# First attention: the keys' exponentials straight from PSUM, head by head, with the bound as bias

## What is computed

```python
def _feature_map(t, K):
    f = jnp.einsum('hdf,bhld->bhlf', K, t)
    feats = jnp.concatenate([jax.nn.softmax(f, axis=-1), jax.nn.softmax(-f, axis=-1)], axis=-1)
    return jnp.maximum(feats, EPS)          # EPS = 1e-12
q, k, v = _heads(x @ Wq), _heads(x @ Wk), _heads(x @ Wv)   # 16 heads of 64
qf, kf = _feature_map(q, Kq), _feature_map(k, Kk)
kv = jnp.cumsum(kf[:, :, :, None, :] * v[..., None], axis=2)
o = jnp.einsum('bhlf,bhldf->bhld', qf, kv)
z = jnp.einsum('bhlf,bhlf->bhl', qf, jnp.cumsum(kf, axis=2)) + EPS
y = (o / z[..., None]) ... @ Wo
```

## Time and profile before

| | |
|---|---|
| median of 3 runs | 1234.21 us (1233.17 to 1234.81) |
| the profiled execution | 1229.25 us, its span 1227.0 us |
| busy over the span | PE 1117.3 (91%), DVE 962.1 (78%), ACT 611.1 (50%), GpSimd 377.3 (31%) |
| granted TensorE clock, mean | 0.982 |
| first attention, tiles 0 to 15 | about 53 to 540 us |

### The profile page before, as it was taken

The page is one execution under the profiler, slowest core; times in us unless marked ns, Lnnn a source line. Parts: engine busy times, 40 slices in busy tenths (PEclk is TensorE's granted clock), DMA queues, the critical chain, the costliest instruction groups (busy, mean ns, idle before and its releaser), DMA issues. The chain is left out here.

```text
span 1227.0 us, 30062 instructions
## 1 busy us (share of the span) xinstructions
PE 1117.3 (91%) x11860; PEld 719.6 (59%) x11861; DVE 962.1 (78%) x1769; ACT 611.1 (50%) x1166; POOL 377.3 (31%) x355
## 2 busy tenths in 40 slices
PE   6698898899899999879999999999999957999996
PEld 5577777777788878643443344334444334666765
DVE  6889978987888788888788677877889556777757
ACT  4233343334333433227777677776788822444443
POOL 4432245222522222113201320222110414656651
PEclk9899999999999999999999999999999988999998
DMA  7100001000400000524720570065050144221225
GB/s 240 41 8 1 2 28 53 2 1 1 80 2 2 1 1 2 81 59 81 152 34 8 114 146 2 9 127 108 2 211 3 53 80 145 65 64 60 63 62 205
DMA packets 60045, 73.65 MB, mean 60 GB/s; under 512 B 14404, under 2 KB 51140, under 8 KB 59188
## 3 DMA queue, kind: packets, MB, share of 16 engines
q1 hardware_dynamic: 56132, 61.56, 21.0%
q0 software_dynamic: 3792, 10.36, 2.7%
HBM read 52.86 MB, written 18.78 MB: 58 GB/s over the span
## 5 line engine op out<-in xcount | busy, mean ns | idle before, releaser
L1791 DVE TENSOR_REDUCE neg_max<-pS 128x1 f32<-128x1024 f32 x238 | 284.9, 1220 | 56.2 <-PE pS L1574 56.0
L1706 ACT ACTIVATE pt<-pR 128x512 f32<-128x512 f32 x512 | 286.5, 600 | 80.1 <-PE pR L1597 75.3
L1597 PE MATMUL pR<-qs,ks 100*32 100x512 bf16 x2048 | 191.2, 383 | 3.1 <-ACT pt L1706 1.6
L1574 PE MATMUL pS<-ks,qs 100*32 100x512 bf16 x1904 | 145.9, 381 | 5.1 <-issue 1.9
L1611 PE MATMUL b_pO<-pt,b_v 128*32 128x512 f32 x1024 | 135.9, 605 | 2.9 <-ACT pt L1706 2.3
L1597 PEld LDWEIGHTS pR<-qs,ks 100*32 100x32 bf16 x2048 | 56.2, 96 | 95.3 <-issue 25.6
L324 POOL TENSOR_TENSOR kf<-kf,fsum 128x2048 f32<-128x2048 f32 (+1 forms) x17 | 58.2, 3422 | 163.8 <-DVE fsum L933 163.8
L324 POOL TENSOR_TENSOR qs<-qs,fsum 128x2048 f32<-128x2048 f32 (+1 forms) x17 | 58.5, 3446 | 142.7 <-DVE fsum L933 142.7
L1453 POOL COPY qs<-max_rows 3x512 bf16<-3x512 bf16 x60 | 36.6, 610 | 209.3 <-ACT max_rows L1699 206.3
L745 ACT COPY qfT<-pT 128x512 f32<-128x512 f32 x64 | 37.3, 582 | 122.7 <-PE pT L466 122.7
L1574 PEld LDWEIGHTS pS<-ks,qs 100*32 100x32 bf16 x1904 | 51.4, 97 | 74.3 <-issue 35.7
(11 more groups left out here) (376 smaller groups left out, 2270.8 us busy)
## 6 DMA issues: line engine op xcount, KB each, us to landing
qs<-q_scr SPq DMA_DIRECT2D x24, 256.0 KB
ks<-k_scr SPq DMA_DIRECT2D x7, 768.0 KB
k_scr<-f SPq DMA_DIRECT2D x18, 256.0 KB, 2.8
ks<-in_L_ffn_w_dram SPq DMA_DIRECT2D x2, 2048.0 KB, 11.1
ks<-in_L_ffn_w_dram SPq DMA_DIRECT2D x4, 1024.0 KB, 8.5
ks<-y_rows SPq DMA_DIRECT2D x16, 256.0 KB, 5.1
ks<-k_scr SPq DMA_DIRECT2D x6, 512.0 KB
cx<-in_ctx_dram SPq DMA_DIRECT2D x3, 768.0 KB, 12.3
```

The costliest lines, as they stand in the source:

```text
L1574: ins = pe.matmul(pS1[q:q + XV, slot, 512 * half:512 * half + 512], qs[0:KR, bass.ds(par, 1), h, P * t + q:P * t + q + XV].rearrange("r a ...
L1597: ins = pe.matmul(ring[bank][q:q + XV, :], ks[0:KR, bass.ds(par, 1), h, P * j + q:P * j + q + XV].rearrange("r a n -> r (a n)"), qs[0:KR, ...
L1706: nc.scalar.activation(pt[:, j % 2, i, :], ring[bank], ACT.Exp).then_inc(exp_done, 1)
L1791: nc.vector.tensor_reduce(neg_max[:, hg % 2, u // G, u % G:u % G + 1], pS1[:, u % 2, :], AX_X, ALU.max, negate=True).then_inc(max_done, 1)
```

## The change

ACT reads the keys' projections from PSUM and takes exp(f - max) and exp(min - f) itself: one instruction for each head and sign, on 128x64, with the negated maximum or the minimum of the head as the bias of each row. That is 32 instructions for a tile in place of two, in four parts of eight. DVE only takes the bounds (`key_bounds`) and shifts no keys. `project_q` waits for the exponentials in place of the shift. In ACT's order part 0 stands where the first half was, part 1 behind `f_copies(t+1, 0)`, part 2 right behind it, and part 3 behind `f_copies(t+1, 1)` of the next tile.

The keys' denominators move, on DVE, from the end of a tile to g = 1 of the next one (where the clamp was), the keys' clamp moves behind `normalise_o` of g = 2, and GpSimd scales keys and queries of the same tile one behind the other.

```diff
@@ GpSimd @@
-                scale(0, 1, 1)
...
                         if not (last and c == TB - 1):
+                            scale(0, TB * b + c + 1, (c + 1) % 2)
                             scale(1, TB * b + c + 1, (c + 1) % 2)
...
-                        if not (last and c >= TB - 2):
-                            scale(0, TB * b + c + 2, c % 2)
@@ PE @@
                 def project_q(t, half, par):
-                    wait(pe, shifted[0], 2 * t + half + 1)
+                    wait(pe, expd[0], 2 * t + half + 1)
@@ ACT @@
+                def key_exponentials(t, part, par):
+                    half = part // 2
+                    wait(act, shifted[0], 2 * t + half + 1)
+                    wait(act, o_done, 4 * (t - 1))
+                    f = pP[:, 512 * half:512 * half + 512] if t else FIRST_K[half]
+                    for h in range(G * part, G * part + G):
+                        col = HD * (h - 8 * half)
+                        nc.scalar.activation(feat[0][:, par, h, 0:HD], f[:, col:col + HD], ACT.Exp,
+                                             bias=hi[:, 0, h:h + 1])
+                        ins = nc.scalar.activation(feat[0][:, par, h, HD:F2], f[:, col:col + HD], ACT.Exp,
+                                                   bias=lo[:, 0, h:h + 1], scale=-1.0)
+                    if part % 2:
+                        ins.then_inc(expd[0], 1)
...
                         f_copies(t, 1)
+                        if has1:
+                            key_exponentials(t + 1, 3, 1 - par)
...
                         if has2:
-                            exponentials(0, t + 2, 0, par)
+                            key_exponentials(t + 2, 0, par)
                         if has1:
                             f_copies(t + 1, 0)
                         if has2:
-                            exponentials(0, t + 2, 1, par)
+                            key_exponentials(t + 2, 1, par)
+                            key_exponentials(t + 2, 2, par)
@@ DVE @@
+                def key_bounds(t, half):
+                    hs = slice(8 * half, 8 * half + 8)
+                    f = pP[:, 512 * half:512 * half + 512] if t else FIRST_K[half]
+                    f = f.rearrange("p (h f) -> p h f", h=H // 2)
+                    wait(dve, proj[0], 2 * t + half + 1)
+                    nc.vector.tensor_reduce(hi[:, 0, hs], f, AX_X, ALU.max, negate=True)
+                    nc.vector.tensor_reduce(lo[:, 0, hs], f, AX_X, ALU.min).then_inc(shifted[0], 1)
...
-                shift(0, 0, 0, 0, own)
+                key_bounds(0, 0)
...
-                shift(0, 1, 1, 1, own)
+                key_bounds(1, 1)
...
-                denominators(0, 1, 1, own)
...
                             if g == 1 and has1:
-                                clamp(0, t + 1, 1 - par)
+                                denominators(0, t + 1, 1 - par, own)
                             if c < TB - 1:
                                 update(b, c, g)
                             if g == G - 1 and has2:
                                 x_rest(t + 2, par)
                             normalise_o(t, g, own)
+                            if g == 2 and has1:
+                                clamp(0, t + 1, 1 - par)
...
                         if has2:
-                            shift(0, t + 2, 0, par, own)
-                            shift(0, t + 2, 1, par, own)
-                            denominators(0, t + 2, par, own)
+                            key_bounds(t + 2, 0)
+                            key_bounds(t + 2, 1)
```

More of the change, by code:

```diff
@@ L162, in linear_attention @@
         v_proj, v_copied = sem("v_proj"), sem("v_copied")
-        shifted = [sem("k_shifted"), sem("q_shifted")]
+        shifted = [sem("k_bounds"), sem("q_shifted")]
         expd = [sem("k_exp"), sem("q_exp")]
@@ L212, in linear_attention @@
         WARM = 16
-        DVE_BATCH = 72
+        DVE_BATCH = 56
         HALVES = (slice(0, H // 2), slice(H // 2, H))
@@ L607, in first_v @@
                     pe.wait_ge(wv_split, 2 * half + 2)
-                    pe.wait_ge(shifted[0], 1)
+                    pe.wait_ge(expd[0], 1)
                     project(2, half, 0, v_proj, FIRST_V[half])
@@ L784, in _ @@
                 w_t_copy(5)
-                exponentials(0, 0, 0, 0)
+                key_exponentials(0, 0, 0)
+                key_exponentials(0, 1, 0)
                 w_copy(4)
                 w_t_copy(6)
-                exponentials(0, 0, 1, 0)
+                key_exponentials(0, 2, 0)
+                key_exponentials(0, 3, 0)
                 w_copy(5)
@@ L797, in _ @@
                 v_copy(0, 1, 0)
-                exponentials(0, 1, 0, 1)
+                key_exponentials(1, 0, 1)
                 f_copies(0, 0)
-                exponentials(0, 1, 1, 1)
+                key_exponentials(1, 1, 1)
+                key_exponentials(1, 2, 1)
                 def batch(b, last):
@@ L907, in _ @@
                 statistics(2)
+                def key_bounds(t, half):
[5 more added lines that the diff above has]
+                    nc.vector.tensor_reduce(lo[:, 0, hs], f, AX_X, ALU.min).then_inc(shifted[0], 1)
                 def shift(m, t, half, par, own):
                     hs = slice(8 * half, 8 * half + 8)
-                    f = pP[:, 512 * half:512 * half + 512] if t else (FIRST_K, FIRST_Q)[m][half]
+                    f = pP[:, 512 * half:512 * half + 512] if t else FIRST_Q[half]
                     f = f.rearrange("p (h f) -> p h f", h=H // 2)
@@ L1046, in turned_maxima @@
                                               pA[:, :, :].rearrange("p h n -> p (h n)")[XV * q:XV * q + 3, 0:TB * 64].bitcast(BF16))
-                shift(0, 0, 0, 0, own)
+                key_bounds(0, 0)
                 w_rest(3)
-                shift(0, 0, 1, 0, own)
+                key_bounds(0, 1)
                 w_rest(4)
@@ L1067, in _ @@
                 clamp(1, 0, 0, HALVES[0], 0)
-                shift(0, 1, 0, 1, own)
+                key_bounds(1, 0)
                 clamp(1, 0, 0, HALVES[1], 1)
-                shift(0, 1, 1, 1, own)
+                key_bounds(1, 1)
                 dve.wait_ge(s_k, 6)
                 mask(0, 0)
-                denominators(0, 1, 1, own)
                 before = own.n
```

## The result

| | before | after |
|---|---|---|
| median of the runs timed side by side | 1233.69 us (1227.18 to 1234.81) | 1283.88 us (1280.87 to 1291.06) |
| the profiled execution, its span | 1229.25, 1227.0 us | 1282.78, 1280.7 us |
| granted TensorE clock, mean | 0.982 | 0.960 |

The kernel became slower: the ratio on record is 1.0427, with a 95% interval of 1.037 to 1.0484 (the two medians by themselves give 1.041). The forecast was 1272.2 us in a range of 1244 to 1288. The sign, the place and the mechanism came as forecast; the loss is 50 us where 38 were reckoned, and most of the difference is a term that the sum did not have.

What follows compares the result with a forecast made beforehand. DVE was taken to bound each tile's middle, PE its tail. The profiled 1229.25 us plus 35.4 (stage) and 2.6 (prologue) gave 1267.3; with 4.96 for the runs' median, 1272.2 us, range 1244 to 1288.

Steps and rivals of the forecast that it cites:

- Who sets which part of the tile: Each tile: DVE sets the middle, PE the tail; work taken from DVE's tail gains at most 8.0 us over the stage.
- tail: From the keys' projection to the next scores of group 1: set by PE, continuous but for 0.40 us in tile 10.
- middle: From `mask(1)` to the keys' projection: 16.3 us in tile 10, set by DVE working back to back.
- The middle, tile by tile: Added time per tile: 3.1 us in tiles 6, 9, 10, 13, 14, other amounts elsewhere; sum 43.4 us.
- The clamp under GpSimd's scaling: Keys' clamp behind `normalise_o(2)` waits out GpSimd's scaling, ends about 1 us later; `update(3)` starts 3.1 us later in tile 10.
- ACT's price: One small 128x64 activation on ACT every 0.20 us, bounds 0.06 and 0.35; a part of eight takes 1.6 us.
- Rival 2: Small ACT activations cost more, deciding from 0.26 us each: 1293 us at 0.31, 1309 at 0.35; 8 in 100.
- The prologue: Ahead of the tiles: ACT's longer exponentials +4.5 us, DVE freed earlier -1.3, bounds and a part -0.6; net +2.6 us.
- Rival 1: Keys' clamp is not held and runs beside GpSimd's scaling: +13.2 us, 1247.4 us; 10 in 100.
- Rival 3: Faster: PE sets the middle, so denominators there cost nothing and the masks' 8.0 us are gained: 1228.8 us; 8 in 100.
- Rival 4: Whole kernel: no change that can be told, the masks' gain equalling the middle's loss; 4 in 100.

Runs made afterwards that it cites:

- The last two experiments: Against the kernel after: clamp in tail, tile 0's old shift, second half's key sums at g = 1 (1.0032); then ACT also sums the last part (0.9973).
- the kernel with the fill: Kernel after plus sixteen unused PE transposes ahead of the keys' projection in tiles with c < 3: 1264.31 us, ratio 1.0264.
- The order alone: Kernel before with only the new DVE and GpSimd order; DVE still shifts keys, ACT takes half-tile exponentials: 1279.39 us, ratio 1.0378.
- each half's denominators where its time is: Kernel after with first-half key sums in the tail, second-half at g = 1, clamp in tail, tile 0's old shift: 1233.56 us, ratio 1.0032.

## Why the prediction was right, and where it was not

- **Who sets which part of the tile.** Right. What left DVE's tail gave next to nothing, and what came into its middle was paid for in full. In a tile without a fall of the clock the tail went from 12.96 to 12.33 us: 0.63, where 0.40 was forecast. PE's waits for the mask ahead of the scores went from 8.8 us in the stage to 0.6, as counted. Fourteen tails of 12.33 would be 172.6 us, 11.8 below the 184.4 of before, where 8.0 were called the most. Of that 3.8, 14 x 0.23 is what a tail gained beyond its wait: in tile 10 the first matmul of these scores started 11.80 us behind the projection before and 11.24 after, and the second 11.99 and 11.35. So a PE wait of 0.40 by its idle mark cost 0.64. By line up to 600 us (busy us, mean ns, idle before), one row of the kernel before and two of the kernel after:

```profile
L436 PE MATMUL pP<-wk_lo,a_xT_hi 128*128 128x512 f32 x60 | 26.8, 446 | 15.1 <-DVE a_xT_lo L884 13.2 <-ACT v L738 1.1 <-DVE qs L921 0.8
...
L473 PE MATMUL pA<-qfT,kfT 128*128 128x128 f32 x512 | 69.0, 279 | 2.5 <-ACT kfT L758 2.0 <-DVE am L971 0.6
...
L434 PE MATMUL pP<-wk_lo,a_xT_hi 128*128 128x512 f32 x60 | 30.5, 508 | 37.5 <-DVE a_xT_lo L903 35.6 <-ACT v L751 1.1 <-DVE qs L949 0.8
```

  The waits did not vanish, they moved and grew: PE waits 35.6 us for `a_xT_lo` where it waited 13.2, and ahead of the state's matmuls 29.4 us where it was 14.0.
- **The middle, tile by tile.** Right, and nearly to the figure. Tiles 6, 9, 10 and 13: 3.1 forecast, 3.09 measured in each. Tiles 0 and 12: 3.6, measured 3.55 and 3.56. Tile 1: 4.3 and 4.23; tile 2: 5.1 and 5.14; tile 5: 2.6 and 2.64; tiles 4 and 8: 2.9, measured 3.23 and 2.89; tiles 3, 7 and 11: 1.3, 1.4, 0.2, measured 1.56, 1.79, 0.26. The sum is 41.2 for 40.3.
- **The clamp under GpSimd's scaling.** Right: 3.24 us, ending 1.08 behind the scaling where 0.96 was reckoned from line 999, and GpSimd's own 3.62 unchanged. The two experiments on it (clamp moved away, scaling moved away) both bring 1.22 us back in tile 10, so this is shown, not inferred. The rule of the Trainium skill (SBUF — State Buffer, section "SBUF: two separate sides"), by which the shared ports belong to one instruction at a time, agrees with the trace for this shape too.
- **ACT's price.** Right: 0.20 us was taken, 0.197 is measured. In the kernel after, behind the bounds of tile 10:

```profile
428.21 0.41 ACT L739 ACTIVATE kf<-pP,hi 128x64 f32<-128x64 f32 x1
428.42 0.41 ACT L741 ACTIVATE kf<-pP,lo 128x64 f32<-128x64 f32 x1
...
431.16 0.52 ACT L741 ACTIVATE kf<-pP,lo 128x64 f32<-128x64 f32 x1
```

  Sixteen of them start in 2.95 us, 15 steps of 0.197. Rival 2 did not come, and the 0.24 that was worked out from the Trainium skill (ScalarE: Activation LUTs, section "What ACT_TABLE_LOAD costs") is not borne out at this shape.
- **The prologue.** The mechanism came, and its size was short: +4.1 for +2.6. Each of tile 0's two exponentials became 16 steps, 22.68 to 25.83 = 3.15 us for the first (3.2 forecast; compare). ACT in the prologue of the kernel after:

```profile
22.68 0.33 ACT L739 ACTIVATE kf<-pO,hi 128x64 f32<-128x64 f32 x1
...
25.83 0.72 ACT L716 CAST w_hi<-pP 128x512 fp32r<-128x512 f32 x1
...
29.73 0.59 ACT L741 ACTIVATE kf<-pDW,lo 128x64 f32<-128x64 f32 x1
```

  PE's first projection of the queries (at 31.57) waited 2.91 us for the weights, where it had waited 0.70 (at 27.58), and the windows of that time show a low clock:

```profile
22.00:28.00 6.00, 3.60 (x31) 3.30 (x30) 1.99 (x5) 6.00 (x27) 5.84 (x4) 1.00 0.33 121
28.00:36.00 8.00, 4.84 (x19) 3.78 (x18) 4.50 (x20) 3.98 (x16) 3.77 (x3) 0.57 0.01 3
```

  Before the change 28 to 36 us had a clock of 1.00, but a low one came later: over the first 62 us the mean is 0.92 before and 0.89 after. How much of the 1.5 us is the clock stays open. The start of the first `mask(1)` differs by one to two microseconds between kernels with one and the same prologue, and in these pairs it is later where the clock was lower. The last two experiments have 60.16 us at a mean clock of 0.83 over the first 62, and 58.10 at 0.89. The kernel after has 61.86 at 0.89, the kernel with the fill 63.07 at 0.83. The order alone, with the old exponentials, has 59.71 at 0.86, the kernel before 57.80 at 0.92.
- **The missing term.** The sum took PE's work in a tail as a fixed 12.9 us, for a clock that stood at 1.00 in all windows read. The change makes PE wait 2.63 us ahead of the tails of tiles 9, 10 and 13, where tile 10 had 0.92, and 7 of the 14 tails (1, 2, 4, 5, 8, 9 and 12) had part of their time at 1.2 GHz. The tails are 185.9 us in place of those 172.6: **13.3 us**. Tile 14 took 2.5 more than forecast, the prologue 1.5, the middles 0.9; the tails' own larger gain, 3.8, stands against them, and 13.3 + 2.5 + 1.5 + 0.9 - 3.8 = 14.4, the miss in the stage. Tile 14's 2.5 look like the same term: its mean clock is 0.90, a fifth of 34.55 us at 1.2 GHz, where it was 1.00 before, and the kernel with the fill, at 0.95, takes 1.97 less for it. The fill experiment gave 10.3 us of the stage back, with the middles as they were. As what could break it the prediction named a clamp, activations and a middle that come out otherwise. It had no price for a wait of PE beyond its length: that was the step that failed.
- **Rivals.** Rival 1 fell with the scaling that waits. Rival 3 fell with the middles. Rival 4 fell with the result.

## What to carry to other kernels

Ahead of taking work off an engine, find the stretch of the period in which that engine sets the pace: work taken from elsewhere gains little, and the reordering that comes with it may put more into the stretch than left. Ask of each DVE operation from SBUF to SBUF with a scalar what GpSimd does at that moment, since it can cost the rest of GpSimd's instruction. And reckon a longer wait of PE at more than its length: the clock of the work behind it may fall too, and matmuls that do nothing can be cheaper than the wait, as sixteen of them were here.

## What the runs showed of the hardware

- **The clock.** With the same work and the same wait of 2.63 us ahead of it, tile 9's tail saw the clock fall and tile 13's did not. Nor is one wait's length the measure: before the change tile 5's tail had a wait of 2.67 us ahead of it and no fall, and with each half's denominators where its time is (ratio 1.0032), tile 1's tail had a mean clock of 0.84 with a wait of only 0.93 ahead of it. Over the stage as a whole PE was busy for 414.51 of 453 us (62 to 515) before, at a mean clock of 1.00, and for 436.57 of 506 us (62 to 568) after, at 0.95. When a fall comes these runs don't explain. The Trainium skill (TensorE: Matmul & The Clock Gate, section "Part 1: The HAM clock gate") lets the clock go by how busy PE has been of late; the trace agrees in the direction.
- **Durations of small activations.** In a long row of them the profile's duration of one grows, from 0.33 to 0.59 us in the prologue and to 400 ns in the mean over the stage, while one still starts every 0.197 us. So the cost is read from the starts. The group of line 739 in the stage:

```profile
L739 ACT ACTIVATE kf<-pP,hi 128x64 f32<-128x64 f32 x240 | 89.9, 396 | 6.5 <-DVE lo L935 6.5
```

- **A sum with an activation** is a second instruction, ACTIVATION_READ_ACCUMULATOR, and makes one come every 0.29 us in place of 0.197.
- **A held operation** of DVE lasted 3.24 us by its own record; DVE's next instruction began 0.07 us before its recorded end, so all of the hold was passed on to what stood behind it.
